# Gated cross attention block: the two fp32 score passes written as 32x32 tiles of TensorE

## What is computed

```python
def _L0_xattn_ref(values, keys, query, mask, ...):
    v = (values @ Wv + bv).reshape(N, -1, H, D)
    k = (keys @ Wk + bk).reshape(N, -1, H, D)
    q = (query @ Wq + bq).reshape(N, Lq, H, D)
    energy = jnp.einsum('nqhd,nkhd->nhqk', q, k)
    energy = jnp.where(mask == 0, neg, energy)
    attn = jax.nn.softmax(energy / jnp.sqrt(D), axis=-1)
    out = jnp.einsum('nhqk,nkhd->nqhd', attn, v).reshape(N, Lq, E)
    return out @ Wo + bo

x = x + jnp.tanh(g_xattn[0]) * _L0_xattn_ref(ctx, ctx, _layernorm(x), mask, ...)
x = x + jnp.tanh(g_ffn[0]) * tanh(_layernorm(x) @ W1 @ W2 @ W3 + b_ffn)
```

## Time and profile before

| | |
|---|---|
| time, median of 3 runs | 1119.73 us (1119.67 to 1120.63) |
| span of the profiled execution | 1118.3 us |
| TensorE matmul busy | 1073.6 us (96%), 18979 matmuls |
| VectorE busy | 966.1 us (86%) |
| ScalarE busy | 826.3 us (74%) |
| GpSimd busy | 774.2 us (69%) |
| mean granted TensorE clock | 0.988 |

### The profile page before, as it was taken

The page is one execution under the profiler, slowest core; times in us unless marked ns, Lnnn a source line. Parts: engine busy times, 40 slices in busy tenths (PEclk is TensorE's granted clock), DMA queues, the critical chain, the costliest instruction groups (busy, mean ns, idle before and its releaser), DMA issues.

```text
span 1118.3 us, 45477 instructions
## 1 busy us (share of the span) xinstructions
PE 1073.6 (96%) x18979; PEld 941.8 (84%) x18979; DVE 966.1 (86%) x1272; ACT 826.3 (74%) x1275; POOL 774.2 (69%) x1185
## 2 busy tenths in 40 slices
PE   5989999999999999999999999999999999999975
PEld 4777888888888888888888888888888888888865
DVE  4788888988988988898888898898889889889876
ACT  4465877877887787787777787778778778777842
POOL 5245677777777776776777777777777777777653
PEclk9899999999999999999999999999999999999997
DMA  6134344334434433433433443443443344343232
GB/s 167 30 89 117 77 120 136 102 106 134 110 114 119 128 107 107 135 108 98 136 103 104 136 108 112 123 124 106 112 135 106 102 135 108 113 121 108 71 116 77
DMA packets 160189, 124.78 MB, mean 112 GB/s; under 512 B 91889, under 2 KB 126962, under 8 KB 159986
## 3 DMA queue, kind: packets, MB, share of 16 engines
q1 hardware_dynamic: 159842, 121.61, 38.8%
q10 hardware_dynamic: 144, 0.26, 0.1%
HBM read 69.41 MB, written 51.38 MB: 108 GB/s over the span
## 4 chain that ended last, share of the span: by engine, by line
PE 89%; DVE 5%; issue 2%; SPq 2%; DMA 1%; ACT 0%; DVEq 0%
PE ps_m L455 17%; PE ps_m L448 16%; PE ps_s L573 13%; PE ps_s L546 12%; PE ps_x L585 11%; PE ps_m L510 8%; PE ps_m L442 5%; PE ps_s L552 4%; PE ps_x L563 2%; DVE neg_max L938 2%; DVE probs L949 2%; DMA a_rows<-scratch_a 0%; DMA den<-a_den 0%; SPq L200 0%; PE ps_m L598 0%
## 5 line engine op out<-in xcount | busy, mean ns | idle before, releaser
L949 DVE TENSOR_TENSOR probs<-ps_s,far_T 128x2048 f32<-128x2048 f32 x128 | 293.3, 2292 | 36.8 <-PE ps_s L573 36.6
L938 DVE TENSOR_REDUCE neg_max<-ps_s 128x16 f32<-128x2048 f32 x128 | 291.3, 2276 | 6.4 <-PE ps_s L552 6.3
L748 ACT ACTIVATE probs<-probs 128x2048 f32<-128x2048 f32 x128 | 244.5, 1910 | 7.9 <-DVE probs L949 7.7
L723 ACT ACTIVATE q_aug<-ps_m,q_bias,q_scale 128x256 f32<-128x256 f32 x256 | 123.7, 564 | 161.9 <-PE ps_m L448 152.4
L573 PE MATMUL ps_s<-q_aug,k_aug 32*128 32x128 f32 x4096 | 152.8, 284 | 7.4 <-DVE neg_max L938 3.3
L546 PE MATMUL ps_s<-k_aug,q_aug 32*128 32x128 f32 x4096 | 151.1, 284 | 6.4 <-DVE probs L949 6.1
L573 PEld LDWEIGHTS ps_s<-q_aug,k_aug 32*128 32x128 f32 x4096 | 129.9, 187 | 27.2 <-issue 17.4
L944 DVE TENSOR_TENSOR q_aug<-q_aug,ps_x 128x512 f32<-128x512 f32 x128 | 88.0, 687 | 74.0 <-PE ps_x L563 74.0
L546 PEld LDWEIGHTS ps_s<-k_aug,q_aug 32*128 32x128 f32 x4096 | 126.9, 187 | 28.3 <-issue 28.3
L585 PE MATMUL ps_x<-probs,v_ones 128*32 128x128 f32 x4096 | 139.2, 277 | 3.9 <-issue 2.3
L388 POOL TENSOR_TENSOR y<-y,th 128x512 f32<-128x512 f32 x58 | 74.1, 1278 | 88.7 <-ACT th L769 88.7
(11 more groups left out here) (122 smaller groups left out, 1958.2 us busy)
## 6 DMA issues: line engine op xcount, KB each, us to landing
scratch_a<-a_den SPq DMA_DIRECT2D x64, 512.0 KB, 3.1
x_in<-in_x SPq DMA_DIRECT2D x64, 256.0 KB, 3.7
a_rows<-scratch_a SPq DMA_DIRECT2D x64, 256.0 KB
den_wide<-scratch_r SPq DMA_DIRECT2D x64, 256.0 KB
out<-y SPq DMA_DIRECT2D x64, 256.0 KB, 5.3
ctx_in<-in_ctx SPq DMA_DIRECT2D x252, 64.0 KB, 3.8
den<-a_den SPq DMA_DIRECT2D x128, 8.0 KB
scratch_r<-den_r SPq DMA_DIRECT2D x64, 16.0 KB, 1.4
```

Of the source, the lines that this page charges most:

```text
L723: last = nc.scalar.activation(dst[:, :, 2 * m + a, :], src[:, m * TOK:(m + 1) * TOK].rearrange("p (n q) -> p n q", q=P), ACT.Identity, bia ...
L748: nc.scalar.activation(tile, tile, ACT.Exp).then_inc(probs_ready, 1)
L938: nc.vector.tensor_reduce(out_v, ps_s[:], AX.X, ALU.max, negate=True).then_inc(max_ready, 1)
L949: nc.vector.tensor_tensor(probs[i % 2][:].rearrange("p j s q -> p (j s) q"), ps_s[:].rearrange("p j s q -> p (j s) q"), far_T[:].unsqueeze ...
```

## The change

Each matmul of a score pass is split by its 128 weight columns into four, c = 0 to 3, each at `tile_position=(j * ROWS, c * ROWS)`: weights 32 x 32, the same moving 32 x 128, output 32 x 128 on partitions 32c to 32c + 31 of bank j. A pass now has 64 matmuls in the program (128 in the trace, with 128 weight loads), in eight rounds of sixteen. The order is c outside, j inside. Nothing else changes: not the waits, not the order of the stages, no other engine's list.

```diff
                 for s in range(SLOTS):
-                    for j in range(G):
-                        rows = slice(j * ROWS, (j + 1) * ROWS)
-                        nc.tensor.matmul(ps_s[:, j, s, :], q_aug[p % 2][rows, n, s, :], k_aug[p % 2][rows, n, s, :],
-                                         start=(s == 0), stop=False, tile_position=(j * ROWS, 0), skip_group_check=True)
+                    for c in range(G):
+                        part = slice(c * ROWS, (c + 1) * ROWS)
+                        for j in range(G):
+                            rows = slice(j * ROWS, (j + 1) * ROWS)
+                            nc.tensor.matmul(ps_s[part, j, s, :], q_aug[p % 2][rows, n, s, part], k_aug[p % 2][rows, n, s, :],
+                                             start=(s == 0), stop=False, tile_position=(j * ROWS, c * ROWS), skip_group_check=True)
...
                 for s in range(SLOTS):
-                    for j in range(G):
-                        rows = slice(j * ROWS, (j + 1) * ROWS)
-                        last = nc.tensor.matmul(ps_s[:, j, s, :], k_aug[p % 2][rows, n, s, :], q_aug[p % 2][rows, n, s, :],
-                                                start=True, stop=True, tile_position=(j * ROWS, 0))
+                    for c in range(G):
+                        part = slice(c * ROWS, (c + 1) * ROWS)
+                        for j in range(G):
+                            rows = slice(j * ROWS, (j + 1) * ROWS)
+                            last = nc.tensor.matmul(ps_s[part, j, s, :], k_aug[p % 2][rows, n, s, part], q_aug[p % 2][rows, n, s, :],
+                                                    start=True, stop=True, tile_position=(j * ROWS, c * ROWS))
```

## The result

The changed kernel takes 1544.47 us (median of four runs, 1540.54 to 1550.92) beside 1119.7: a ratio of 1.380, 95% interval 1.376 to 1.384. It is 425 us slower. The forecast of 1118.6 with a range to 1138 is far off, and two of its rivals, A (a pass is longer) and B (the supply of instructions), have both come true at several times their price.

A forecast was written before the change was run, and what follows sets the result against it. A loop of `turn_max`, VectorE's chain up to the maxima, second pass and projections was taken to bound the kernel; +0.3 - 0.8 - 0.6 = -1.1 us gave 1118.6 us, range 1110 to 1138.

The forecast's parts named there:

- A: Rival, chance 0.23: rounds of a score pass stretch, slower; +6 us at a round of 0.120 us, +18 us at 0.135.
- B: Rival, chance 0.12: a pass can't be shorter than its instruction packet of 1.2 us; second passes cost 38 us, 1157.
- The cover of 0.13 us: Beside VectorE's chain: a first pass longer by less than 0.13 us costs nothing.
- Point 1: Start of a pass: loads of 32 columns bring the second round after 0.135 us instead of 0.215, gain 0.08.
- Point 2: Rounds of a pass: issuing sixteen pairs at 6.7 ns takes 0.107 us and just fits under a 0.112 us round.
- The upper bound of 0.135 a round: Rounds of a pass: at most one exposed 32-column load, 0.026 us, is added to each round.
- Point 3: End of a pass: the last round's starts take 0.10 us instead of 0.02, a loss of 0.08.
- Point 4: First pass into mask step: 0.13 us a batch gained, of which only 0.8 and 0.6 us reach the time.
- C: Rival, chance 0.03: a row group's four column tiles take turns; pass 3.6 us, kernel some 690 us more.
- D: Rival, chance 0.06: pairs start every 3.3 ns, faster; pass 0.84 us, -8 us, 1110.
- E: Rival, chance 0.04: the gain at the mask step reaches the path after all, up to -17 us, 1102.
- little or nothing happens: Forecast case, chance 0.52: 0.42 within 0.2% and 0.10 just under it; its likeliest range is 1116 to 1120.

## Why the prediction was wrong

**What bounds the kernel** was read rightly: the second pass is on the path, and the first lies beside VectorE's chain (shown by the kernel without the mask step, within 12 us instead of 5). The cover of 0.13 us was just far too small for what came.

**Point 1, the start of a pass,** held: 0.133 us from the first matmul to the seventeenth, against 0.135.

**Point 2, the rounds, is the step that failed.** "A round of sixteen must also be issued: at 6.7 ns for a pair" took the spacing of the first four matmuls of the earlier trace rows and of the burst of the earlier trace rows as the rate at which TensorE can be fed. Both are, beside the long runs, best read as instructions that had been issued ahead and were waiting. The rate at which they come in over 128 or 256 is 4.0 ns each, 8.0 a pair, measured with bf16 in steps of 128 and of 256 instructions. At that rate alone the pass is 1.02 us instead of 0.905; with fp32 it is 1.63, and the 0.61 us between are measured but not explained. The upper bound of 0.135 a round, one exposed load, was no bound: the measured pace behind the first two rounds is 0.47 / 2 = 0.23. No row before showed a sustained rate above one instruction in 14 ns (as rival B itself said), so nothing there allowed the range to end at the load.

**Point 3, the end of a pass,** is lost in point 2. **Point 4:** the gap of 0.2 us into the mask step is indeed gone, and no change of data type brings it back. The first mask matmuls stand among the last of the pass; windows of L554 around the end of a pass whose last matmul starts at 815.385:

```profile
815.26:815.39 0.13, 0.12 (x5) 0.12 (x8) 1.00 0.00 0
815.26:815.56 0.30, 0.29 (x16) 0.27 (x16) 1.00 0.00 0
```

So "TensorEngine Tiling (Array Packing)" of the Trainium skill, that changing the mode drains and changing the tile doesn't, agrees with both traces. But the mask step then takes 0.275 us instead of 0.05, and its gain is nothing beside a first pass that is 0.73 us longer.

**Rival A** had the right direction and a price of +18 us at most; its size was 202 + 28. Its cause, loads that aren't pulled ahead, was not the one for the 1.02 us that issue alone takes; for the other 0.61 no run excludes it. **Rival B** had the right mechanism at 0.12, was priced at 38 us and cost 195. Its two arguments against were both wrong: the average of 5.3 packets a turn says nothing where 352 instructions stand together, and the 0.05 us burst wasn't a supply. Its price took the packet's own 1.2 us; a block needs 2.5 us from its packet's start, and the packet begins only after the boundary before. Of the two statements in "Runtime: NRT & Kernel Launch" of the Trainium skill (Instruction fetch mechanics), the traces agree with the two blocks for TensorE: a packet begins behind the boundary before it in all but one of 343. That it has room for eight no run here shows. C, D and E did not happen. The fall of the clock, some 25 us, stood in no point and in no rival.

The weights were wrong too: with two unmeasured quantities in the same step, issue at 3.4 ns an instruction and four times the instructions in a pass, 0.52 for "little or nothing happens" rested on bursts of 32.

## What to carry to other kernels

Splitting a matmul by its weight columns into more tiles doesn't use more of the array if the tiles before already filled it; it only multiplies instructions. Count instructions as a resource of TensorE, with two prices: at 4.0 ns each (fp32 at sixteen tiles: 6.4) they must fit under the streaming (128 did, 256 did not, and fp32's come in twos), and any 256 in a row that are used up in under some 3 us mostly meet a gap at the block boundary, those that last 4 us sometimes. Gaps of 2 us cost a second time, in the stages behind them, when TensorE's clock falls. A burst in a trace that follows a wait is no rate: look for the longest run of instructions with no wait ahead of it.

## What the runs showed that I had not expected

- TensorE needs 4.0 ns for each bf16 load or matmul over a long run of them (1.016 us for 256, 0.510 for 128), and fp32 on sixteen tiles, behind the first 32 matmuls, 0.47 us for each 16 of two parts, 7.3 ns an instruction.
- "Idle, released by issue" of 1 to 2.5 us in a matmul stream, at a multiple of 256 instructions, is the instruction fetch; it took 197 us of 1549 in the changed kernel and 4 of 1118 in the one before.
- Such gaps also bring the granted clock down to 1.2 GHz: 88 us of it, with a cost of some 25, where the kernel before had none behind its first 60 us and before its last 50.
- The four-tile layout with bf16 operands is at 1042.93 us faster than both kernels: a pass of 0.19 us instead of 0.905. It isn't the same computation, the scores have bf16 operands; and it waits for VectorE before the second pass 119 times, 45.5 us, so not all of 1.4 us a batch reached the time.
